# Heads of 64: the products with V one step behind the transposes, a second set of transposed probabilities, the output in the ring of banks 6 and 7

## The reference

```python
q = (x @ Wq).reshape(B, Nq, HEADS, DIM_HEAD)
k = (context @ Wk).reshape(B, context.shape[1], HEADS, DIM_HEAD)
v = (context @ Wv).reshape(B, context.shape[1], HEADS, DIM_HEAD)
sim = jnp.einsum('bihd,bjhd->bhij', q, k) * SCALE
attn = jax.nn.softmax(sim, axis=-1)
out = jnp.einsum('bhij,bjhd->bihd', attn, v)
return out.reshape(B, Nq, HEADS * DIM_HEAD) @ Wo + bo
```

## Time and profile before

| what | value |
|---|---|
| median of three runs | 3782.75 us |
| the profiled execution: its own time, its span | 3780.22 us, 3778.5 us |
| PE matmul busy | 3292.9 us, 87% |
| DVE, ACT, POOL busy | 2124.1, 1587.3, 1281.5 us |
| mean granted PE clock | 0.944 |
| L2_xattn | about 2097 to 2325 us |
| L3_attn | about 2478 to 2925 us |
| L3_xattn | about 2925 to 3365 us |

### The profile page before, as it was taken

One profiled execution on the slowest core, in us unless ns is written; L12 is line 12 of the kernel. 1 busy time (PEld: TensorE's weight loads), 2 busy tenths in 40 slices (PEclk: granted clock), 3 DMA queues, 4 the chain that ended last, 5 costly groups with the idle time before them and its releaser, 6 DMA issues. The chain is left out here.

```text
span 3778.5 us, 60584 instructions
## 1 busy us (share of the span) xinstructions
PE 3292.9 (87%) x23021; PEld 2615.6 (69%) x23021; DVE 2124.1 (56%) x4511; ACT 1587.3 (42%) x3697; POOL 1281.5 (34%) x1019
## 2 busy tenths in 40 slices
PE   6977799999789688589898898979998899989998
PEld 4544688888655355489555676857776677769998
DVE  4643355555556356457554464557776555556555
ACT  3541122221145355255354454335555555544554
POOL 2100100101111177277333433033333433336996
PEclk9988799999899799799899899999999999999999
DMA  1001100000000000054000101011000000005663
GB/s 53 2 2 49 38 17 17 33 17 0 20 2 3 21 1 1 1 203 172 26 2 2 41 5 45 1 39 42 1 1 1 35 5 5 1 23 181 218 220 113
DMA packets 53063, 156.99 MB, mean 42 GB/s; under 512 B 13394, under 2 KB 31586, under 8 KB 40404
## 3 DMA queue, kind: packets, MB, share of 16 engines
q1 hardware_dynamic: 49076, 143.42, 11.0%
q0 software_dynamic: 3744, 10.23, 0.9%
HBM read 142.58 MB, written 10.26 MB: 40 GB/s over the span
## 5 line engine op out<-in xcount | busy, mean ns | idle before, releaser
L1715 POOL TENSOR_TENSOR prob<-prob,inv 128x512 f32<-128x512 f32 x320 | 331.9, 1042 | 639.1 <-DVE inv L1756 632.8
L1641 ACT ACTIVATE prob<-bank,nmax 128x256 f32<-128x256 f32 x640 | 297.8, 474 | 66.2 <-DVE nmax L1750 66.2
L1750 DVE TENSOR_REDUCE nmax<-bank 128x2 f32<-128x512 f32 x320 | 219.7, 688 | 136.9 <-PE bank L1620 132.2
L2786 ACT ACTIVATE hf<-bank 128x512 f32<-128x512 f32 x128 | 76.7, 599 | 398.7 <-PE bank L2729 398.7
L2302 DVE TENSOR_REDUCE nmax<-bank 128x2 f32<-128x512 f32 x256 | 164.4, 684 | 115.0 <-PE bank L2016 115.0
L2729 PE MATMUL bank<-xH,upH 128*128 x512 | 201.6, 394 | 18.2 <-POOL upL L2798 18.2
L2729 PE MATMUL bank<-xL,upH 128*128 x512 | 200.6, 392 | 0.0
L2729 PE MATMUL bank<-xH,upL 128*128 x512 | 200.2, 391 | 0.0
L2798 POOL TENSOR_TENSOR upL<-W,upH 128x2048 fp32r<-128x2048 f32 x8 | 36.8, 4601 | 469.6 <-ACT upH L2763 469.6
L2826 DVE TENSOR_TENSOR hf<-bank,hf 128x512 f32<-128x512 f32 x128 | 88.5, 692 | 160.1 <-PE bank L2729 160.1
L2187 ACT ACTIVATE probT<-bank 128x512 f32<-128x512 f32 (+1 forms) x258 | 131.2, 563 | 91.2 <-PE bank L2135 51.3
(11 more groups left out here) (489 smaller groups left out, 10746.8 us busy)
## 6 DMA issues: line engine op xcount, KB each, us to landing
W<-in_L_ffn_experts SPq DMA_DIRECT2D x80, 1024.0 KB, 5.5
W<-in_L_ffn_experts SPq DMA_DIRECT2D x8, 1536.0 KB, 7.8
slots_y<-W SPq DMA_DIRECT2D x23, 256.0 KB, 6.3
W<-strips SPq DMA_DIRECT2D x4, 768.0 KB, 6.7
cs<-in_ctxT SPq DMA_DIRECT2D x20, 128.0 KB, 2.4
W<-in_L_ffn_experts SPq DMA_DIRECT2D x9, 256.0 KB, 4.8
X<-in_x SPq DMA_DIRECT2D x1, 2048.0 KB, 8.7
W<-in_L_ffn_experts SPq DMA_DIRECT2D x1, 2048.0 KB, 7.6
```

What stands on the lines that cost most here:

```text
L1641: ins = nc.scalar.activation(m_.prob[p % 2][:, e * 512 + j * S:e * 512 + (j + 1) * S], bank(key)[:, j * S:(j + 1) * S], ACT.Exp, bias=m_.n ...
L1715: nc.gpsimd.tensor_tensor(pr, pr, m_.inv[:, slot(p, e):slot(p, e) + 2].unsqueeze(2).to_broadcast([P, 2, S]), ALU.mult)\
L1750: nc.vector.tensor_reduce(m_.nmax[:, slot(p, e):slot(p, e) + 2], sc, AX.X, ALU.max, negate=True).then_inc(g.max_ready.sem, 1)
L2786: nc.scalar.activation(out, src_, ACT.Silu).then_inc(g.freed[u.bank(key)].sem, 1)
```

## The change

The products get a lag of their own, O_AT = 4, and the output projection moves to lag 5. On PE the products of pair s - 4 stand where those of pair s - 3 stood. `probT` becomes two sets, taken in turn by the parity of the pair; the second set lies over the raw weights of K, which are read only while they are split into high and low parts in the first steps. The products leave bank 3 and take their place in the ring of banks 6 and 7, so banks 3 and 4 hold transposes alone. ScalarE's copy to `OT` follows the new lag; the order on each engine stays, and each stage has one step more.

```diff
-        self.probT = [sb("probT0", 512), sb("probT1", 512)]
+
+        self.probT = [[sb("probT0", 512), sb("probT1", 512)], [raw["k"][:, 0:512], raw["k"][:, inner:inner + 512]]]
@@
-    S_AT, X_AT, T_AT, Y_AT = 1, 2, 3, 4
+    S_AT, X_AT, T_AT, O_AT, Y_AT = 1, 2, 3, 4, 5
@@
-        p, _, _ = pair(s, T_AT)
+        p, _, _ = pair(s, O_AT)
         if p is not None:
-            u.add(("O", p), 3)
+            misc(("O", p))
@@
-                p, b, i = pair(s, T_AT)
+                p, b, i = pair(s, O_AT)
                 if p is not None:
                     if i % 4 == 0:
                         freed(pe, ("V", b, i // 2)), freed(pe, ("V", b, i // 2 + 1))
@@
-                            mm = nc.tensor.matmul(to[64 * e:64 * e + 64, 0:S], m_.V[b % 2][:, vc:vc + 64], m_.probT[e][:, kt * S:(kt + 1) * S],
+                            mm = nc.tensor.matmul(to[64 * e:64 * e + 64, 0:S], m_.V[b % 2][:, vc:vc + 64], m_.probT[p % 2][e][:, kt * S:(kt + 1) * S],
@@
-                    copy(("T", t, 1), m_.probT[1][:, :], 512)
+                    copy(("T", t, 1), m_.probT[t % 2][1][:, :], 512)
@@
-                if t is not None:
-                    copy(("O", t), m_.OT[:, :], S)
+                o, _, _ = pair(s, O_AT)
+                if o is not None:
+                    copy(("O", o), m_.OT[:, :], S)
@@
-                    copy(("T", t, 0), m_.probT[0][:, :], 512)
+                    copy(("T", t, 0), m_.probT[t % 2][0][:, :], 512)
```

## The result

The changed kernel took 3694.9 us (median of 4 runs, 3688.9 to 3705.8), the kernel before 3782.4 beside it: a ratio of 0.9769, with a 95% interval of 0.9749 to 0.9790, that is 79 to 95 us less. 3702.5 was forecast. The profiled execution took 3688.9 us, its span is 3687.2.

A forecast was written before the change was run, and what follows sets the result against it. PE sets the pace, leaving 110 us open, with waits before products and V projection. Terms 42 + 5.9 + 29 - 2.8 + 9.6 - 3.8 = 80 us gave 3700 us profiled, 3702.5 median; range 3690 to 3715, 75%.

The forecast's parts named there:

- (a): Plain steps: products one step later no longer wait for VectorE's copy of the transposes; 42 us gained over the three stages.
- (b): Batch closing moves into the V step with the later output projection, so V's late starts go; 29 us gained.
- (c): Plain step after a closing: products wait for qL, 0.5 us in context stages; L3_attn gains 5.9 us, charged 2.8.
- the list of signs: Expected in the profile after: among others, PE's wait for qL at the products, about 0.5 us long, 14 times.
- (d): Products' output in the ring of banks 6 and 7: all claims met with 1.1 us or more, cost 0.
- (e): Other engines' chains (GpSimd scalings, score banks, VectorE's copy) still finish in time at the shorter step; cost 0.
- (g): Fill: step 3 loses its products, step 4 its projection; 3.2, 3.5 and 2.9 us for the stages, 9.6 gained.
- (h): Drain: one more projection and product pair at each stage's end; 1.6, 0.8 and 1.4 us lost, 3.8.
- A: Rival: VectorE is the next to be late, each of 20 closings costs 1 us more; 3722 us, 14%.
- B: Rival: the closing holds products as long as it held V, so (b) is void; 3731 us, 5%.
- C: Rival: claims of the two-bank ring wait for other engines and slow PE; 3863 us at 1 us a step, 2%.
- D: Rival: PE's granted clock falls to the 1.2 GHz level for a fifth of its busy time; about 3903 us, 1%.

The follow-up runs named there:

- e4: Changed kernel with the output back in bank 3, lags and second set of transposed probabilities kept: 25.5 us slower than the kernel before, ratio 1.0068.
- e1: Kernel before with only the output projection moved to lag 5 (two OT buffers), products still at lag 3 in bank 3: 16.7 us slower, ratio 1.0037.
- e2: Changed kernel with the output projection at lag 6 (two OT buffers): 40.0 us faster than the kernel before, ratio 0.9894.
- e3: Kernel before with only the products' output moved to the ring of banks 6 and 7: 4.0 us faster, ratio 0.9989 (interval reaches past 1).
- e7: Changed kernel with two extra ScalarE copies in front of each copy to OT: 55.3 us faster than the kernel before, ratio 0.9856.
- e8: Changed kernel with four extra ScalarE copies in front of each copy to OT: 66.8 us slower than the kernel before, ratio 1.0176.
- e5: Changed kernel with VectorE's normalisation of a closed batch moved to the end of its step: 85.6 us faster than the kernel before, ratio 0.9778.
- f2: Changed kernel with the normalisation at the end of VectorE's step, run once more: 87.1 us faster than the kernel before, ratio 0.9764.
- f1: The changed kernel itself, run again on another chip: 84.7 us faster than the kernel before, ratio 0.9775.
- e9: Changed kernel with the normalisation at the end of the following V step (lag Y_AT + 2): 87.6 us faster than the kernel before, ratio 0.9769.

## Why the prediction was right

**(a), the plain steps.** Right to 0.03 us: 5.27 and 5.28 against 5.26 and 5.3. e4 shows what the prediction said only in passing: the bank was as needed as the lag.

**(b), the moved closing.** Right in size: V steps of 6.64 to 6.67 instead of 8.37 and 7.69. But I gave the 29 us to the closing's new place as if it were a term by itself. e1 shows that alone it loses 17 us, because products that wait for VectorE's copy meet the delay in place of V; e2 shows that without it the changed kernel is 45 us slower. (In both runs some of this, 7 and 12 us, is the lower clock behind the long waits.) The two parts are worth their sum only together.

**(c), the next wait.** Its place and its cause were right, and so were the 13 closings of the context stages (the list of signs said 14). The products are 0.37 us late where 0.51 was computed: the residual sum starts 0.07 us sooner, and from there to the products 5.53 us pass instead of 5.63. The bias sum took 0.84 us instead of 1.05 (the rows above), with a GpSimd scaling beside it for 0.30 us instead of 0.50. By the rule of the Trainium skill (SBUF — State Buffer, Who interferes with whom) that sum could gain up to 0.35 us; it gained 0.21, of which 0.10 reached the products. In L3_attn 0.2 instead of 0.1 us, and the V step behind it 7.27 instead of 7.11, 0.16 late where I charged 0.4.

**(d) and (e), bank and chains.** Cost 0: e3 shows it for the ring before the change, e7 and e8 measure the slack, which behind a closing is 0.2 us and not 1.1.

**(g), the fill.** The first eight steps (with the first plain waits) lost 4.3, 8.1 and 3.1 us; my terms for them add up to 4.3 (3.2 and 1.1), 6.5 (3.5 and 3.0) and 4.0 (2.9 and 1.1). Without the 1.5 us of the DMA wait L3_attn's loss is 6.6.

**(h), the drain.** The table's last row, less the products' wait of that step, which (a) counts, gives losses of 0.7 us for L3_attn and 1.7 for L3_xattn: right (0.8 and 1.4). For L2_xattn it gives 3.2 + 0.6 = 3.8, where 1.6 was charged. This is the term that was mis-sized. It counted a product pair and a projection of 1.0 us each in the tail, the pace of the middle. The end of L2_xattn in the changed kernel:

```profile
2293.77 1.09 PE L1578 MATMUL bank<-ident,prob 128*128 128x128 f32 x4 [3.89 <-POOL prob L1717]
...
2296.05 1.91 PE L1598 MATMUL bank<-W,OT 128*128 128x256 f32 x4
...
2297.89 1.98 PE L1611 MATMUL bank<-probT,W 128*64 128x256 f32 x8
...
2300.35 1.13 PE L1598 MATMUL bank<-W,OT 128*128 128x256 f32 x4 [0.48 <-ACT OT L1635]
```

The closing of the last batch but one now stands later in the drain and holds the maxima, the exponential and GpSimd's scaling, so PE is idle for 3.89 us. Behind that it runs at half the clock (0.50 granted from 2293.7 to 2300.0, the 1.2 GHz level): a projection 1.91 us instead of 1.03, the products 1.98 instead of 1.08, 1.8 us in all. But the drain before the change had such a gap and a shorter stretch of that kind too, at its products:

```profile
2312.94 1.66 PE L1610 MATMUL bank<-probT,W 128*64 128x256 f32 x8 [3.63 <-DVE probT L1738]
```

By the starts of its groups that one cost 1.5 us. So the clock alone does not make up the 2.2 us missed. The place of the normalisation has a share: where it stands later (e5, f2, the same code) the last transposes of this stage wait 2.34 us instead of 3.89, and the row of the table is 22.9 and 24.1 us instead of 25.6. How the 2.2 us divide stays open.

**The rivals.** A (VectorE next) did not come: it asked for 1 us a closing beyond (c), and a closing costs less than (c) has, 0.37 us for 0.51 in the context stages and 0.37 for 0.5 in L3_attn, both its steps counted. B: e1 is its case, with the products kept where they were. Of its arguments one was misread: the closing starts not 1.2 but 0.14 us earlier against the next step (6.67 - 4.9 = 1.77 us ahead of it for 3215.22 - 3213.59 = 1.63). What saved the 29 us is that products are due 1.04 us later in their step than V. C did not come; e8 shows it where its slack is used up. D did not come either: the changed kernel's stages stayed at 0.96 to 0.99, one more user of the ring notwithstanding. The clock fell behind waits of 1.8 to 2.5 us in e1, e2 and e4, at 24 of their 60 closings, and not once behind the waits of 0.5 to 1.5 us in the stages before the change.

**The remainder.** 9.4 us of the profiles' difference lie in code that was not changed. Three profiles on one chip, f1, f2 and e9, have their first Q of L2_xattn at 2109.2, 2106.3 and 2101.9 us, with the same code ahead of it: this part varies by some 7 us between executions. So the 81.9 of the stages is the better measure of the change. That its sum is within 2% of the forecast is in part luck: L3_attn gave 3.2 us more than its terms, L2_xattn 1.2 less.

## What to carry to other kernels

Write down one step of the busiest engine, start by start. Its steps without gaps give the pace the others would have, and two subtractions gave the gain of a stage to within 1 to 3 us here. A wait goes only if the data and the memory that it stands for are both free: a lag without a bank, or a bank without a lag, gained nothing here. Work that comes once in several steps (norms, closings) should be placed by what is claimed behind it; moving it on its own engine was worth 28 us with no other change.

## What the runs showed of the hardware

- PE's clock fell to its 1.2 GHz level behind some waits of 1.8 to 2.5 us and not behind others of the same length: at 7 of 20 closings in e1 (waits of 2.4 us), 8 of 20 in e2 (1.8 to 2.0) and 9 of 20 in e4 (2.4). A step behind such a wait then took up to 1.6 us more (e2: 10.99 for 9.39). A median over steps hides this.
- In the drain of L2_xattn the same code (e5, f2) had the same wait of 2.34 us and was at the lower level for 3.4 and for 6.8 us; the drains differ by 1.2 us.
- VectorE's normalisation from SBUF (two operations) took 0.74 us with GpSimd idle and 1.53 beside its scaling.
- The kernel before took 27 to 33 us more in the three later groups of runs, while the three dense stages of the changed kernel, run again, agreed to 0.2 us, and its first Q came 17 us later. That this is the chip is not shown.
